# A graph network kernel on one core: the row stores of its three table stages move from GpSimd's DMA queue to SyncE's, behind the loads there

## The chip, the cores and the metric

The kernel runs on one core of a Trainium2 chip. A core has five engines with an instruction queue each: TensorE (PE in the profile), VectorE (DVE), ScalarE (ACT), GpSimd (POOL) and SyncE (SP), and 16 DMA engines that all queues share. SP only issues transfers. The metric is the device time of the kernel in microseconds (us), as the median of several runs.

## The reference

Nodes have rows of 128 numbers. Two relational layers and one attention layer work on the same 400,000 edges, which are sorted by destination. Cut to what matters here:

```python
h = relu(layernorm(x))                        # 12500 x 128
# two layers; relation = argmax of 10 columns of edge_attr
mean[n, r] = mean over edges (src -> n, relation r) of h[src]
h1 = relu(sum_r mean[n, r] @ w_rel1[r] + h @ root1 + b1)
x = x + (the same with h1, w_rel2, root2, b2)
h = relu(layernorm(x))
xl, xr = h @ W_l, h @ W_r
score = leaky_relu(xl[src] + xr[dst]) . att   # 4 heads
x = x + softmax over the edges of dst (score) * xl[src] + bias
```

## The kernel before

The kernel multiplies before it gathers. A table stage (`tables`, L372) computes for each node row all products that edges can ask of it, and an edge pass then gathers one 128-number row of that table per edge. The order of the program is: preparation, `tables("t1")`, edge pass p1, `tables("t2")`, edge pass p2, `tables("t3")`, score pass, softmax weights, `attend`, `finish`. Each is a block of its own, and all engines meet at a barrier between blocks.

A table stage goes over 98 tiles of 128 node rows, in 49 pairs. In a pair number j, buffer k (0 or 1) serves tile i = 2j + k. Every buffer of the stage exists twice, one for even and one for odd tiles: the loaded rows `xt` (t_x in the trace), the normalized rows `hn` (t_hn), their transpose `ht` (t_ht), the product `py` in PSUM (t_py), and the table rows `yb` (t_y) that are stored to HBM. Each engine runs its own stream of instructions, and semaphores tie them together:

- SP loads the rows of x (L420). In t1 the load of tile i waits for the normalized rows of tile i-2 (L489, semaphore s_hn). In t2 it waits for the last addition of tile i-2 (L521, s_yd), since x is added there. In t3 nothing is loaded. SP instead saves x after the relational layers, which lies in A, to `x1_dram` (L440).
- DVE, in its pair j, first makes the rows of pair j+1: statistics (L473, t1 and t3, which in t1 wait for the load), L477, L481, and the normalized rows L489 (in t2 a plain relu, L492). Then, for the two tiles of pair j, it copies the last 256 columns of the product into yb (L511, t1 and t2) and writes A (L516, or L519 and L521, or L514). Before the copy into yb[k] it waits for the store of tile i-2 out of it (s_out).
- ACT takes the square roots (L545), copies the first 1024 columns of the product into yb (L561, all 128 columns in t3; it waits for the same store), and writes ht with a relu (L551).
- PE multiplies tile i (L590, three matmuls of up to 512 columns in t1 and t2, the trace shows each as two), then transposes tile i+2 (L581). A product waits for both copies of tile i-2.
- POOL only issues the stores (L454): tile i goes out when both ACT's and DVE's part of it is done (s_ya and s_yd). A store is 640 KB in t1 and t2 (128 rows of 5,120 bytes) and 64 KB in t3.

A wait on SP or POOL is written as `gate(...)`, and its instructions appear at L81 and L82, lines of that helper. Instructions of one queue are taken in order, so a wait holds up everything behind it.

Of the kernel before, what the change touches and what calls it, by code (L numbers as in the profile page):

```python
# [24 lines left out]
ds = bass.ds  # L25

P = 128
# [7 lines left out]
NT = -(-N // P)  # L35
LAST = N - (NT - 1) * P
# [24 lines left out]
def build(nc, x, src, dst, attr, w_rel1, root1, b1, w_rel2, root2, b2, w_l, w_r, att, bias, out,  # L61
# [3 lines left out]
    def sem(name):  # L65
        return outer.enter_context(nc.semaphore(name))

    def sbuf(stack, name, shape, dt=F32):
        return stack.enter_context(nc.sbuf_tensor(name, shape, dt))
# [6 lines left out]
    def gate(eng, name, *waits):  # L76

        if name not in passed:
            passed[name] = sem(f"gate_{name}")
        for s, v in waits:  # L80
            eng.wait_ge(s, v)  # L81
        eng.sem_inc(passed[name])  # L82

    def load(eng, kind, table, at, n, top):

        _, values = nc.values_load_multi_w_load_instructions(
            table[0:1, ds(at, n)], engines=[kind], min_val=0, max_val=top,
            skip_runtime_bounds_check_because="the tables are clamped where they are made")
        return values
# [20 lines left out]
    with outer:  # L110
# [261 lines left out]
        def tables(name, first, norm, wcols, load_w, bias_in, save_x1):  # L372
# [3 lines left out]
            dest = ytab if nt > D else xltab  # L376
            with ExitStack() as st:
# [8 lines left out]
                yb = [sbuf(st, f"{name}_y{k}", [P, nt]) for k in range(2)]  # L386
# [3 lines left out]
                s_x = [sem(f"{name}_x_in{k}") for k in range(2)]  # L390
# [4 lines left out]
                s_ya, s_yd = sem(f"{name}_copied_act"), sem(f"{name}_copied_dve")  # L395
                s_add = sem(f"{name}_added")
                s_out = [sem(f"{name}_stored{k}") for k in range(2)]
                s_x1 = sem(f"{name}_x1_stored")
                uses_x = first or bias_in is not None
# [9 lines left out]
                def a_tile(i):  # L409
                    return A[:, ds(i * D, D)]  # L410

                with nc.Block() as block:  # L412

                    @block.sync
                    def _(sp):
                        n_w = load_w(sp, wt, brow, s_w)

                        def load(j, k, rows=P):
                            i = 2 * j + k
                            sp.dma_start(xt[k][0:rows, :], x[ds(i * P, rows), :]).then_inc(s_x[k], 16)  # L420

                        def use(j, k):

                            return (s_hn if first else s_yd, 2 * j + k - 1)

                        if uses_x:
                            load(0, 0)
                            load(0, 1)
                            with sp.Fori(1, NT // 2 - 1) as j:
                                for k in range(2):  # L430
                                    gate(sp, "sp", use(j, k))
                                    load(j, k)
                            j = NT // 2 - 1
                            for k in range(2):
                                gate(sp, "sp", use(j, k))
                                load(j, k, P if k == 0 else LAST)
                        elif save_x1:
                            def save(j, k):
                                i = 2 * j + k
                                sp.dma_start(x1_dram[ds(i * P, P), :], a_tile(i)).then_inc(s_x[k], 16)  # L440
                            save(0, 0)
                            save(0, 1)
                            with sp.Fori(1, NT // 2) as j:
                                for k in range(2):

                                    gate(sp, "sp", (s_x[k], 16 * j))
                                    save(j, k)

                    @block.gpsimd
                    def _(pool):  # L450
                        def store(j, k):
                            i = 2 * j + k
                            gate(pool, "pool", (s_yd, i + 1), (s_ya, i + 1))
                            pool.dma_start(dest[ds(i * P, P), :], yb[k][:, :]).then_inc(s_out[k], 16)  # L454
                        with pool.Fori(0, NT // 2) as j:
                            for k in range(2):
                                store(j, k)
                        for k in range(2):
                            pool.wait_ge(s_out[k], 16 * (NT // 2))
                        if save_x1:  # L460
                            for k in range(2):
                                pool.wait_ge(s_x[k], 16 * (NT // 2))

                    @block.vector
                    def _(dve):
# [614 lines left out]
        def finish():  # L1080
            B = 7
            with ExitStack() as st:
# [10 lines left out]
                with nc.Block() as block:  # L1093
# [26 lines left out]
                    def _(dve):  # L1120
# [5 lines left out]
                        for b in range(NT // B):  # L1126
                            k = b % 2
                            dve.wait_ge(s_x[k], 16 * (b // 2 + 1))  # L1128
                            if b >= 2:
# [9 lines left out]
                                            biasb[:, :].rearrange("p (a d) -> p a d", a=1).to_broadcast([P, B, D]), ALU.add).then_inc(s_r, 1)  # L1139

        tables("t1", True, True, ALL, rgcn_weights(w_rel1, root1, b1), b1, False)
        rgcn_pass("p1", True)
        tables("t2", False, False, ALL, rgcn_weights(w_rel2, root2, b2), b2, False)
        rgcn_pass("p2", False)
        relational.close()
        tables("t3", False, True, 2 * D, gat_weights, None, True)
        sc = sbuf(outer, "scores", [P, TILES * H])
        score_pass(sc)
# [39 lines left out]
```

## Time and profile before

| what | value |
|---|---|
| median of 3 runs | 17781.06 us (17738.27 to 17804.8) |
| span of the profiled execution, first to last instruction | 15531.6 us |
| busy in the span | PE 44%, PEld 38%, DVE 42%, ACT 25%, POOL 67% |
| stage t1 | about 953 to 1265 us of the span |
| stage t2 | about 5370 to 5638 us |
| stage t3 | about 9593 to 9830 us |

The profile gives one execution. Its own total time is not on record, only its span, so the 2249.5 us between the span and the median of the runs lie before the first and after the last instruction that the trace shows. The shares of busy time are means over stages that are limited by different things: POOL's 67% is mostly the issue of the gathers in the edge passes. The three table stages together are some 5% of the span. What the change is worth must be read inside them.

### The profile page before, as it was taken

What the parts mean: (1) busy time and instruction counts of PE and PEld (TensorE: products, weight loads), DVE (VectorE), ACT (ScalarE), POOL (GpSimd) and SP (SyncE); (2) the same over time, 40 slices, a digit from 0 to 9 for tenths busy, and PEclk for the clock granted to TensorE, in tenths of its full rate; (3) what the DMA queues carried; (4) which work ended last, traced back from release to release, by engine and by line L of the source; (5) the groups of instructions that cost most, each with busy time, mean ns of one, the idle gap of its engine ahead of it and who ended that gap; (6) DMA issues with size and microseconds to landing.
All of it is one profiled execution on the core that took longest, in us unless ns stands there. A gap on an engine that the chain in (4) does not pass through costs nothing. (4 is left out here: it accounts for less than half of the span.)

```text
span 15531.6 us, 192165 instructions
## 1 busy us (share of the span) xinstructions
PE 6894.7 (44%) x31138; PEld 5952.3 (38%) x31139; DVE 6488.9 (42%) x10730; ACT 3826.4 (25%) x12681; POOL 10415.9 (67%) x10321
## 2 busy tenths in 40 slices
PE   0055444444444564444444444444444444444776
PEld 0023333333333333333333334333333333334775
DVE  3762222222222231111111112566666666667777
ACT  0023222222222232222222222111111111112554
POOL 0125777777777647777777775577777777773665
PEclk9996555555555675555555555555555555557998
DMA  3132111111111241111111112355555555552555
GB/s 129 54 124 96 50 50 50 50 51 50 50 50 50 83 164 52 52 52 52 52 52 52 52 52 60 106 148 148 148 148 148 148 147 148 148 147 84 163 164 162
DMA packets 683413, 1471.04 MB, mean 95 GB/s; under 512 B 193803, under 2 KB 259975, under 8 KB 676759
## 3 DMA queue, kind: packets, MB, share of 16 engines
q0 software_dynamic: 331360, 749.89, 18.2%
q1 hardware_dynamic: 339288, 714.47, 13.9%
q10 hardware_dynamic: 12738, 6.40, 0.1%
q14 instruction: 20, 0.16, 0.0%
q8 instruction: 7, 0.11, 0.0%
HBM read 1117.48 MB, written 352.52 MB: 95 GB/s over the span
## 5 line engine op out<-in xcount | busy, mean ns | idle before, releaser
L694 POOL DMA_INDIRECT p_g<-ytab,p_i x6250 | 6107.0, 977 | 1927.9 <-issue 1691.3
L672 PE MATMUL p_pg<-p_v,p_oh 128*128 x14480 | 3451.5, 425 | 4609.3 <-ACT p_v L732 3432.4
L672 PEld LDWEIGHTS p_pg<-p_v,p_oh 128*128 128x128 f32 x14480 | 3087.5, 320 | 4974.2 <-issue 4974.2
L694 POOL DMA_INDIRECT a_g<-xltab,a_i x3125 | 3205.4, 1026 | 962.7 <-issue 950.9
L647 DVE TENSOR_TENSOR A<-p_pg,A 128x128 f32 x1448 | 422.6, 292 | 6013.8 <-PE p_pg L672 5880.4
L867 PE MATMUL a_pg<-A,a_oh 128*128 x7240 | 1755.6, 431 | 2430.3 <-DVE a_oh L813 2430.3
L867 PEld LDWEIGHTS a_pg<-A,a_oh 128*128 128x128 f32 x7240 | 1577.8, 326 | 2608.2 <-issue 2607.4
L732 ACT ACTIVATE p_v<-p_g,wgt 128x128 f32<-128x128 f32 x6250 | 1960.4, 389 | 461.2 <-issue 437.1
L726 ACT ACTIVATE p_i<-rel_i 128x5 int32 (+1 forms) x1250 | 260.1, 208 | 5338.1 <-DMA p_g<-ytab,p_i 5338.1
L1072 POOL TENSOR_TENSOR s_v<-s_x,scores 128x512 f32<-128x512 f32 x625 | 798.0, 1291 | 660.7 <-PE s_pg L672 415.0
L633 DVE TENSOR_TENSOR p_oh<-cols,local 128x640 f32<-128x640 f32 x1456 | 1199.1, 824 | 38.0 <-PEq L412 12.6
L672 PE MATMUL s_pg<-s_v,s_oh 128*128 x7240 | 957.0, 291 | 314.6 <-DVE A L647 225.1
L672 PEld LDWEIGHTS s_pg<-s_v,s_oh 128*128 128x128 f32 x7240 | 894.6, 199 | 377.1 <-issue 369.1
L790 ACT ACTIVATE a_i<-src_i 128x5 int32 (+1 forms) x625 | 130.1, 208 | 3318.0 <-DMA a_g<-xltab,a_i 3318.0
L813 DVE TENSOR_SCALAR a_oh<-a_dst,node 128x640 f32 x726 | 422.5, 582 | 1251.6 <-ACT a_z L795 1181.3
L633 DVE TENSOR_TENSOR s_oh<-cols,local 128x640 f32<-128x640 f32 x728 | 831.5, 1143 | 0.3 <-PEq L1008 0.3
L1036 ACT ACTIVATE s_v<-s_x,scores 128x32 f32<-128x32 f32 x2500 | 597.3, 309 | 620.4 <-PE s_pg L672 531.3
L826 DVE TENSOR_TENSOR a_z<-a_pg,a_z 128x640 f32 x724 | 597.1, 825 | 203.2 <-issue 192.1
L847 DVE TENSOR_REDUCE scores<-a_leaky 128x640 f32 x724 | 590.5, 816 | 80.9 <-DVE scores L847 80.9
L590 PE MATMUL t_py<-t_w,t_ht 128*128 128x512 f32 (+2 forms) x1568 | 620.7, 539 | 6.5 <-ACT t_ht L551 0.9
L838 DVE TENSOR_TENSOR a_leaky<-a_leaky,attb 128x640 f32<-128x640 f32 x724 | 562.1, 817 | 0.0
L833 DVE SCALAR_TENSOR_TENSOR a_leaky<-a_z 128x640 f32 x724 | 561.4, 816 | 0.0
(167 smaller groups left out, 3395.9 us busy)
## 6 DMA issues: line engine op xcount, KB each, us to landing
a_dst<-in_dst_dram SPq DMA_DIRECT2D x625, 320.0 KB, 4.0
xj_dram<-a_g SPq DMA_DIRECT2D x625, 320.0 KB, 2.2
s_x<-xj_dram SPq DMA_DIRECT2D x625, 320.0 KB, 3.1
ytab<-t_y POOLq DMA_DIRECT2D x196, 640.0 KB, 3.4
p_g<-ytab,p_i POOLq DMA_INDIRECT x6250, 2.5
ea<-in_edge_attr_dram SPq DMA_DIRECT2D x50, 1312.5 KB
a_g<-xltab,a_i POOLq DMA_INDIRECT x3125
t_x<-in_x_dram SPq DMA_DIRECT2D x194, 64.0 KB, 2.0
```

The source lines that it names most:

```text
L590: last = t.matmul(py[k][:, to:to + e - c], ht[k][:, :], wt[:, c:e], start=True, stop=True)
L633: v.tensor_tensor(onehot[k][:, :].rearrange("p (t n) -> p t n", t=G), cols[:, :].rearrange("p (a n) -> p a n", a=1).to_broadcast([P, G, P] ...
L672: last = t.matmul(pg[k][:, 0:width], onehot[k][:, q * P:(q + 1) * P], V[:, ds(at + q * width, width)], start=(q == 0), stop=(q == G - 1))
L694: pool.indirect_dma_start(gbuf[k][:, q * D:(q + 1) * D], None, rows, bass.IndirectOffsetOnAxis(ap=stage[k][:, q:q + 1], axis=0)).then_inc( ...
L732: last = a.activation(V[:, c:c + D], gbuf[k][:, q * D:(q + 1) * D], ACT.Copy, scale=wgt[:, ds(G * g + q, 1)])
L826: v.tensor_tensor(z[k], pg[k][:, 0:GD], z[k], ALU.add).then_inc(s_add, 1)
L833: v.scalar_tensor_tensor(L[k][:, :], z[k], SLOPE, z[k], ALU.mult, ALU.max).then_inc(s_lk, 1)
L838: v.tensor_tensor(lk, lk, attb[:, :].rearrange("p (a d) -> p a d", a=1).to_broadcast([P, G, D]), ALU.mult).then_inc(s_wt, 1)
L847: v.tensor_reduce(sc[:, ds(col[k] * H, G * H)], L[k][:, :].rearrange("p (t c) -> p t c", c=C), AX, ALU.add).then_inc(s_done, 1)
L867: last = t.matmul(pg[k % 2][:, q * D:(q + 1) * D], onehot[k % 2][:, q * P:(q + 1) * P], A[:, ds(at, D)], start=True, stop=True)
L1036: a.activation(to[:, q, h * C:(h + 1) * C], rows[k][:, q * D + h * C:q * D + (h + 1) * C], ACT.Copy, scale=sc[:, ds(G * H * g + q * H + h, ...
L1072: q.tensor_tensor(to[:, 0:m, 0:D].rearrange("p t (h c) -> p t h c", h=H), rows[k][:, 0:m * D].rearrange("p (t h c) -> p t h c", t=m, h=H), ...
```

## The change

The block of POOL in the table stages goes away. SP issues the same stores, of the same sizes, with the same waits, and its stream is written so: in the loop it takes the two loads (or saves) of pair j, and then the two stores of pair j-1. The waits for the last stores at the end of the stage move to SP too. The loads of x, the saves, and what DVE, ACT and PE do stay as they are.

```diff
+                        def store(j, k):
+                            i = 2 * j + k
+                            gate(sp, "sp", (s_yd, i + 1), (s_ya, i + 1))
+                            sp.dma_start(dest[ds(i * P, P), :], yb[k][:, :]).then_inc(s_out[k], 16)
+
+                        def save(j, k):
+                            i = 2 * j + k
+                            sp.dma_start(x1_dram[ds(i * P, P), :], a_tile(i)).then_inc(s_x[k], 16)
+
+                        last = NT // 2 - 1
                         if uses_x:
                             load(0, 0)
                             load(0, 1)
-                            with sp.Fori(1, NT // 2 - 1) as j:
+                            with sp.Fori(1, last) as j:
                                 for k in range(2):
                                     gate(sp, "sp", use(j, k))
                                     load(j, k)
-                            j = NT // 2 - 1
+                                for k in range(2):
+                                    store(j - 1, k)
                             for k in range(2):
-                                gate(sp, "sp", use(j, k))
-                                load(j, k, P if k == 0 else LAST)
-                        elif save_x1:
-                            def save(j, k):
-                                i = 2 * j + k
-                                sp.dma_start(x1_dram[ds(i * P, P), :], a_tile(i)).then_inc(s_x[k], 16)
+                                gate(sp, "sp", use(last, k))
+                                load(last, k, P if k == 0 else LAST)
+                        else:
                             save(0, 0)
                             save(0, 1)
-                            with sp.Fori(1, NT // 2) as j:
+                            with sp.Fori(1, last) as j:
                                 for k in range(2):
-
                                     gate(sp, "sp", (s_x[k], 16 * j))
                                     save(j, k)
-
-                    @block.gpsimd
-                    def _(pool):
-                        def store(j, k):
-                            i = 2 * j + k
-                            gate(pool, "pool", (s_yd, i + 1), (s_ya, i + 1))
-                            pool.dma_start(dest[ds(i * P, P), :], yb[k][:, :]).then_inc(s_out[k], 16)
-                        with pool.Fori(0, NT // 2) as j:
+                                for k in range(2):
+                                    store(j - 1, k)
+                            for k in range(2):
+                                gate(sp, "sp", (s_x[k], 16 * last))
+                                save(last, k)
+                        for j in (last - 1, last):
                             for k in range(2):
                                 store(j, k)
                         for k in range(2):
-                            pool.wait_ge(s_out[k], 16 * (NT // 2))
-                        if save_x1:
-                            for k in range(2):
-                                pool.wait_ge(s_x[k], 16 * (NT // 2))
+                            sp.wait_ge(s_out[k], 16 * (NT // 2))
+                            if not uses_x:
+                                sp.wait_ge(s_x[k], 16 * (NT // 2))
```

On SP's queue the loop of stage t1 stood so before (the name in brackets is the semaphore waited for; t1_rows is s_hn):

```order
23 L420 ISA [waits t1_rows]
24 L420 DMA t_x<-in_x_dram 128x128
25 L420 ISA [waits t1_rows]
26 L420 DMA t_x<-in_x_dram 128x128
27 L429 REGISTER_ALU
28 L429 COMPARE_AND_BRANCH
```

And so it stands in the changed kernel, whose line 429 is the store (t1_copied_dve and t1_copied_act are s_yd and s_ya):

```order
23 L420 ISA [waits t1_rows]
24 L420 DMA t_x<-in_x_dram 128x128
25 L420 ISA [waits t1_rows]
26 L420 DMA t_x<-in_x_dram 128x128
27 L81 ISA
28 L429 ISA [waits t1_copied_dve,t1_copied_act]
29 L429 DMA ytab<-t_y 128x1280
30 L81 REGISTER_ALU
31 L429 ISA [waits t1_copied_dve,t1_copied_act]
32 L429 DMA ytab<-t_y 128x1280
33 L439 REGISTER_ALU
34 L439 COMPARE_AND_BRANCH
```

Each load of the next turn now stands behind two waits for copies and two stores, where nothing stood between.

In stage t2 the same loop of the changed kernel has the loads waiting for t2_copied_dve (s_yd) of tiles 2j-2 and 2j-1:

```order
46 L420 ISA [waits t2_copied_dve]
47 L420 DMA t_x<-in_x_dram 128x128
48 L420 ISA [waits t2_copied_dve]
49 L420 DMA t_x<-in_x_dram 128x128
50 L81 ISA
51 L429 ISA [waits t2_copied_dve,t2_copied_act]
52 L429 DMA ytab<-t_y 128x1280
```

The store of tile 2j-2 now stands behind a load that waits for tile 2j-1. On POOL's queue the stores had the loop for themselves, which read before:

```order
33 L454 ISA [waits t1_copied_dve,t1_copied_act]
34 L454 DMA ytab<-t_y 128x1280
35 L81 REGISTER_ALU
36 L454 ISA [waits t1_copied_dve,t1_copied_act]
37 L454 DMA ytab<-t_y 128x1280
38 L455 REGISTER_ALU
39 L455 COMPARE_AND_BRANCH
```

These rows are gone, in all three stages, and POOL goes from one edge pass to the next.

## Rows read from the trace of the kernel before

**Rows 1.** The page: span, and ACT's group of copies (busy, mean, idle before)

```profile
span 15531.6 us, 192165 instructions
...
L561 ACT ACTIVATE t_y<-t_py 128x1024 f32<-128x1024 f32 (+1 forms) x294 | 227.7, 775 | 339.8 <-PE t_py L590 192.3 <-DMA ytab<-t_y 143.3 <-DMA xltab<-t_y 2.3
```

**Rows 2.** Windows t1, t2, t3: length, busy PE, PEld, DVE, ACT, POOL; PEclk, DMA, GB/s

```profile
953.00:1265.00 312.00, 265.09 (x686) 118.41 (x686) 145.38 (x584) 146.55 (x293) 52.35 (x98) 0.99 0.59 225
5370.00:5638.00 268.00, 260.80 (x686) 118.21 (x686) 111.81 (x392) 117.04 (x196) 52.17 (x98) 0.99 0.69 263
9593.00:9830.00 237.00, 141.27 (x490) 104.91 (x490) 113.82 (x491) 78.97 (x294) 52.78 (x98) 0.50 0.18 55
```

**Rows 3.** Windows of the same kind in `attend` and in edge pass p2

```profile
14200.00:15000.00 800.00, 605.16 (x4537) 566.57 (x4538) 599.18 (x909) 416.86 (x1982) 508.42 (x397) 0.94 0.55 164
...
6000.00:8000.00 2000.00, 878.40 (x3679) 785.31 (x3678) 382.56 (x736) 564.62 (x1908) 1515.77 (x1590) 0.52 0.19 52
```

**Rows 4.** SP's own waits: for whom, us in total, times, longest

```profile
SPq L82 <- DVE t_hn L489: 217.3, 48, 5.8
...
SPq L82 <- DVE A L521: 191.8, 96, 9.3
```

**Rows 5.** Timeline of one pair in t1: start, us, engine, line, [idle before]

```profile
1102.21 0.61 DVE L489 TENSOR_SCALAR t_hn<-t_x,t_mv 128x128 f32<-128x128 f32 x2 [0.17 <-DVE t_mv L481]
...
1102.85 0.30 PE L581 MATMUL t_pt<-ident,t_hn 128*128 128x128 f32 x1 [0.79 <-DVE t_hn L489]
...
1102.93 0.95 SPq L420 DMA_DIRECT2D t_x<-in_x_dram  x2
...
1103.24 2.60 PE L590 MATMUL t_py<-t_w,t_ht 128*128 128x512 f32 x6
...
1106.05 1.02 ACT L561 ACTIVATE t_y<-t_py 128x1024 f32<-128x1024 f32 x1 [2.42 <-PE t_py L590]
...
1106.74 0.49 DVE L473 BATCH_NORM_STATS2 t_st<-t_x 128x6 f32<-128x128 f32 x2
```

**Rows 6.** DVE lines 516, 519: durations, first, last start; line 514's wait (us, times)

```profile
L516 DVE TENSOR_TENSOR A<-t_py,t_b x98: 280/281/283, 959.7 to 1261.9; 128x128 f32 x94, 128x128 f32<-128x128 f32 x4
...
L519 DVE TENSOR_TENSOR A<-t_py,t_b x98: 280/281/282, 5376.8 to 5634.2; 128x128 f32 x94, 128x128 f32<-128x128 f32 x4
...
  DMA x_dram<-A: 11.4, 11
```

**Rows 7.** Lines 420, 454 and 773: from issue to landing

```profile
DMA to landing us min/median/max: 1.7/2.0/3.8
...
DMA to landing us min/median/max: 1.8/3.2/3.5
...
DMA to landing us min/median/max: 2.2/2.2/2.7
```

**Rows 8.** PE's timeline at the start of t1

```profile
954.82 4.41 PE L590 MATMUL t_py<-t_w,t_ht 128*128 128x512 f32 x6 [0.24 <-ACT t_ht L551]
```

**Rows 9.** Timeline in t2: the copies, the last addition, the stores

```profile
5499.98 1.02 ACT L561 ACTIVATE t_y<-t_py 128x1024 f32<-128x1024 f32 x1 [0.75 <-DMA ytab<-t_y]
...
5500.77 0.29 DVE L521 TENSOR_TENSOR A<-A,t_x 128x128 f32 x1
...
5501.31 3.73 SPq L420 DMA_DIRECT2D t_x<-in_x_dram  x2
...
5501.83 0.53 POOL L454 DMA_DIRECT2D ytab<-t_y  x1 [1.41 <-DVE A L521]
...
5503.39 1.02 ACT L561 ACTIVATE t_y<-t_py 128x1024 f32<-128x1024 f32 x1 [2.21 <-DMA ytab<-t_y]
...
5505.30 1.02 ACT L561 ACTIVATE t_y<-t_py 128x1024 f32<-128x1024 f32 x1 [0.72 <-DMA ytab<-t_y]
```

**Rows 10.** SP's saves in t3: two small windows of its timeline

```profile
9639.99 0.97 SPq L440 DMA_DIRECT2D x_dram<-A  x2
...
9641.81 0.34 SPq L440 DMA_DIRECT2D x_dram<-A  x1
```

## The prediction

> **What bounds the kernel now.** I read the page first, then the windows of the three table stages, then the timeline of one pair in t1 and in t2, and last the waits and landings of the queues. The page gives a span of 15531.6 us [rows 1]; the change touches only the stages t1, t2 and t3, 312, 268 and 237 us long [rows 2], so all of it plays in 5% of the span, and what counts is the time of one pair of tiles there, of which each stage has 49.
>
> In t1, DVE's line 516 starts 98 times between 959.7 and 1261.9 us [rows 6]. That is 302.2/97 x 2 = 6.23 us a pair. The timeline shows what closes the cycle [rows 5]. PE ends the product of an odd tile at 1103.24 + 2.60 = 1105.84. ACT copies it from 1106.05 to 1107.07. DVE is done with its part at once and begins the statistics of the next pair at 1106.74, 0.9 us after the product's end. The same steps one pair earlier give the rest: the first normalized rows are done at 1102.21 + 0.35 = 1102.56, PE waits 0.79 us for them, transposes, and starts the odd tile's product at 1103.24, so 0.68 after them. From statistics to these rows are 2.1 us (1106.74 - 6.26 = 1100.48 for the start one pair earlier, to 1102.56). Sum: 0.9 + 2.1 + 0.7 + 2.6 = 6.3, the measured pair. So the chain of DVE, and behind it PE, bounds t1, and the statistics are on it with nothing to spare. The loads are off it only because SP issues them at 1102.93 and 1103.54, right after the normalized rows, and they land 2.0 us later at the median [rows 7], at 1104.9 and 1105.5, so 1.2 us or more before they are needed.
>
> In t2 a pair takes (5634.2 - 5376.8)/97 x 2 = 5.31 us [rows 6]. Both copies of a tile wait for the store two tiles back: ACT's copies at 5499.98, 5503.39 and 5505.30 are all released by the landing of a store [rows 9], and over the kernel such landings cost ACT 143.3 us [rows 1]. The cycle of one yb buffer is: copy begins, DVE's last addition ends at 5500.77 + 0.29 = 5501.06 (1.1 us), POOL issues at 5501.83 (0.8 us), the store lands (3.2 to 3.5 us [rows 7]), next copy 0.1 later. That is 5.3, the measured pair. So t2 is bound by its stores, and the two buffers run this cycle side by side.
>
> In t3 PE is busy 60% at half the clock, a pair takes 237/49 = 4.8 us, DMA has a share of 0.18 [rows 2], and only 11.4 us are lost to a transfer, a save [rows 6].
>
> **The change in t1.** POOL's two issues a pair, 0.53 us each, go; SP has room for them, since it waits 217.3 us for normalized rows [rows 4]. But the loads of the next pair now stand behind the store of the odd tile, which waits for ACT's copy of it. From the end of the odd product (0):
> - ACT's copy ends at 1.23 (0.21 + 1.02, [rows 5]).
> - SP issues the store 0.37 after its release, as it issues a load at 1102.93 for rows done at 1102.56: 1.60.
> - SP goes round its loop and issues the first load. Two issues within a turn are 0.61 apart (0.95 - 0.34). Across the end of a turn I have 9639.99 + 0.63 = 9640.62 to 9641.81, 1.2 with a small wait in it [rows 10]. I take 1.05: 2.65, and the second load at 3.26.
> - They land after 2.0 at the median, 1.7 at least [rows 7]: 4.65 and 5.26. The store of 640 KB is ahead of them on the same queue; it lands 3.2 after 1.60, at 4.8, so the first load hardly comes before that. I take 4.8 and 5.25.
> - Statistics at 4.9 instead of 0.9. The second tile's load is a little late, which costs 0.1 more.
>
> That is +4.1 a pair: 10.35 us. It hits rows 2 to 48 of the loop, 47 pairs: 47 x 4.1 = +193 us.
>
> PE's clock adds to it. PE is busy 265.09/312 = 85% in t1, at a granted 0.99, which is 2.4 GHz [rows 2]. After the change it would do 0.85 x 6.23 = 5.3 us in 10.35, 51%, with an idle stretch of over 4 us each pair. At 60% in t3 the grant is 0.50 (1.2 GHz) [rows 2], at 44% in p2 0.52, at 76% in `attend` 0.94 [rows 3]. At the lower level the product takes 4.41 us instead of 2.60 [rows 8], and with the slower transpose the pair 2.0 more: 12.35, +6.1. But PE would then be busy some 80% again, which goes with the high clock. So I expect both levels in turn, and the product behind the idle stretch, the one on the chain, mostly at the lower. I take +5.3: **+249 us**; bounds +193 and +287. The Trainium skill says the same of idle gaps while waiting for a DMA (*TensorE: Matmul & The Clock Gate*, HAM oscillation — how this bites in real kernels); no run here has yet shown it in this loop.
>
> **The change in t2.** The loads and stores wait for nearly the same thing, but the store of tile 2j-2 now stands behind a load that waits for the last addition of tile 2j-1. So both buffers' stores go out together. From that addition's end (0):
> - SP issues the load at 0.25 (5501.06 to 5501.31, [rows 9]), the first store at 0.25 + 0.61 = 0.86, the second at 1.5.
> - The first lands after 3.2 [rows 7], at 4.1. The second is moved behind it: two landings stand 1.9 apart (5503.39 and 5505.30 [rows 9]), so at 6.0.
> - Copy 0.1 later, last addition 1.1 later: 7.2.
>
> Against 5.31 that is +1.9 a pair, 47 x 1.9 = **+89 us**. The gain of SP's quicker issue (0.25 against POOL's 0.77) is in it. If a store of SP lands quicker, the nearest row is L773 with 320 KB and 2.2 [rows 7]; 320 KB more at half of the 1.9 gives 3.15, almost the same. Bounds: +1.3 a pair (60 us) to +2.5 (118 us). PE, busy 260.8/268 = 97% of t2 now [rows 2], would be busy 0.97 x 5.31/7.2 = 72%, near `attend`, so I leave its clock.
>
> **The change in t3.** Four issues a pair on SP take 3 x 0.61 + 1.05 = 2.9 of the 4.8 us. The saves of pair j+1 go out about a pair before DVE overwrites their source; they land long before. The cover is 1.9 us; if it were gone, each us of it costs 49. The 11.4 us may come back. I take **0**, -11 to +10.
>
> **The sum.** 249 + 89 + 0 = +338 us on the span of 15531.6, which gives 15870. The span lies 2249.5 below the median of the runs, and I leave that difference alone: 17781 + 338 = 18119, so **18120 us**. Bounds: 193 + 60 - 11 = +242 and 287 + 118 + 10 = +415.
>
> **Rivals.**
> - *The stores gain from the faster queue, and the order costs nothing* (not slower). Place: the yb cycle in t2. The release-to-issue time falls from 0.77 to 0.25 and the landing perhaps by 0.1: -0.6 x 49 = -30 us, 17750. For it: t2 is bound by this cycle. Against it: it needs the even store to leave before the odd tile is done, while the load ahead of it waits for exactly that; it decides only if that wait is shorter than the 0.5 us gained, and the copies of the two tiles stand 1.9 us apart. 4%. The skill's table of issuing engines names Sync for a simple store and calls that path generally faster (*DMA: Bandwidth & Descriptors*, Issuing engine by pattern); by that rule alone the change would be this gain.
> - *Only the issue moves, no time* (17781). SP sits idle enough [rows 4]: 294 issues x 0.34 = 100 us in three stages. It needs the loads in t1 to have over 4 us to spare; they have 1.2. 4%. The same page says under Issuing engines are not separate DMA queues that issuing from several engines saves only sequencer time; by it nothing else would change.
> - *Only one of the two loops suffers*: t2 alone +89 (17870) or t1 alone +249 (18030). 7%.
> - *Both suffer more than I sum*: PE stays at 1.2 GHz in t1 and falls to it in t2 as well (4.41 a product, over 10 us a pair there, +4.5): 287 + 220 = +507, 18290. Against it: at that level PE is busy all the time in t2, which goes with the high grant. 6%.
> - The forecast, both loops longer by +180 to +510: 79%.
>
> **How the numbers follow.** Range: from +180 to +500, 17960 to 18280, which holds the bounds of the sum and some 8 in 10 of the chance. A measurement of this kernel tells about 0.5%, 89 us, from no change. Slower by more than that: the forecast, the heavier case, and nearly all of the one-loop case, 92%. Within it: the two rivals without loss and a light t2 alone, 7%. Faster by over 0.5% would take 89 us out of the stages, which no term gives: 1%.
>
> **What the profile after would show.** In t1, DVE's statistics (L473) wait some 4 us for the landing of t_x in each pair, where now they follow the addition at once; SP's waits name ACT's copy; line 516's first and last start are some 500 to 550 us apart; PEclk lies between 0.5 and 0.9. In t2, two stores are issued 0.6 us apart on SP, ACT's copies wait for their landings, and a pair takes about 7.2 us with PEclk above 0.9. In t3 nothing but the place of the stores changes. Edge passes and `attend` keep their lengths. I am wrong if the loads in t1 land before 1 us, if the two stores of t2 leave apart, or if the gathers, now first on POOL's queue, run otherwise than before.

## The result, and the profile after

The changed kernel takes **18089.25 us** (median of 4 runs, 18044.45 to 18107.5), the kernel before 17759.67 us (4 runs, 17735.79 to 17804.8) beside it. The ratio is 1.0178, 95% interval [1.0157, 1.0200]: slower by 330 us, that is 1.8%, and clear of the noise. Forecast were 18120 us and +338.

The page of the kernel after gives a span of 18105.7 us where [rows 1] have 15531.6. The time of this same execution was 18107.5 us. So nothing to speak of lies around the span, and the 2249.5 us that the prediction put there must be something else; this is taken up with the whole kernels below.

```profile
span 18105.7 us, 191823 instructions
...
ytab<-t_y SPq DMA_DIRECT2D x196, 640.0 KB, 3.0
```

The stores stand in SP's name, and their median time from issue to landing is 3.0 us. The page of the kernel before has 3.4 for the same 640 KB from POOL (the 3.2 of [rows 7] is the median of all stores of that line, with the small ones of t3):

```profile
ytab<-t_y POOLq DMA_DIRECT2D x196, 640.0 KB, 3.4
```

The windows of t1, t2 and t3 show where the time went; columns as in [rows 2]:

```profile
953.00:1558.00 605.00, 373.22 (x686) 161.25 (x686) 149.28 (x584) 146.63 (x293) 0.00 (x0) 0.78 0.31 117
6236.00:6569.00 333.00, 253.89 (x682) 117.39 (x680) 111.04 (x388) 116.48 (x194) 0.00 (x0) 0.99 0.54 212
11183.00:11420.00 237.00, 141.25 (x490) 104.90 (x490) 114.19 (x492) 79.55 (x299) 0.53 (x1) 0.50 0.19 55
```

t1 went from 312 to 605 us at a granted clock of 0.78 for 0.99, t2 from 268 to 333, t3 kept its 237. More exactly by the first and last start of the lines that write A (now L520, L523 and L518; for the first two [rows 6] give 302.2 and 257.4 us):

```profile
L520 DVE TENSOR_TENSOR A<-t_py,t_b x98: 280/281/282, 959.8 to 1554.8; 128x128 f32 x94, 128x128 f32<-128x128 f32 x4
...
L523 DVE TENSOR_TENSOR A<-t_py,t_b x98: 280/281/282, 6239.2 to 6565.3; 128x128 f32 x94, 128x128 f32<-128x128 f32 x4
...
L518 DVE COPY A<-t_py x98: 291/292/293, 11188.5 to 11416.3; 128x128 f32 x94, 128x128 f32<-128x128 f32 x4
```

That is 595.0 us in t1, +293; 326.1 us in t2, +69; 227.8 us in t3, as before.

Why t1 is longer is seen in one pair of its timeline (columns as in [rows 5]):

```profile
1205.43 0.61 DVE L493 TENSOR_SCALAR t_hn<-t_x,t_mv 128x128 f32<-128x128 f32 x2 [0.17 <-DVE t_mv L485]
...
1206.51 4.99 PE L594 MATMUL t_py<-t_w,t_ht 128*128 128x512 f32 x6
...
1211.44 2.53 PE L594 MATMUL t_py<-t_w,t_ht 128*128 128x512 f32 x6
...
1211.70 1.02 ACT L565 ACTIVATE t_y<-t_py 128x1024 f32<-128x1024 f32 x1 [4.70 <-PE t_py L594]
...
1214.11 0.97 SPq L420 DMA_DIRECT2D t_x<-in_x_dram  x2
...
1216.38 0.63 DVE L477 BATCH_NORM_STATS2 t_st<-t_x 128x6 f32<-128x128 f32 x2 [4.00 <-DMA t_x<-in_x_dram]
```

The product that follows the wait runs 4.99 us and ends at 1211.50. ACT's copy ends at 1212.72, SP issues the next loads at 1214.11, and DVE's statistics start at 1216.38 after 4.00 us of waiting for them: 4.88 us after the product's end, where [rows 5] have 0.9. The next product takes 2.53 us. This is one of the longer pairs, 12.79 us from statistics to statistics where the mean of the stage is 12.27. The slow product is not always as slow. In the timeline of the stage the 47 products behind such a wait take 3.88 to 5.03 us, 4.69 in the mean; none takes the 2.60 us of [rows 5].

SP's own waits have changed their names. Normalized rows cost it 217.3 us in [rows 4] and now 5.8. ACT's copy (at the store of the odd tile) and DVE's row of A (at the store of the even tile) have taken their place:

```profile
SPq L82 <- ACT t_y L565: 245.5, 51, 5.5
SPq L82 <- DVE A L520: 206.4, 47, 4.8
...
SPq L82 <- DVE t_hn L493: 5.8, 1, 5.8
```

In t2 the two stores of a pair leave together, the second issue 0.7 us after the first. The second copy of each pair is released by the landing of its store. For the first the profile names PE's product, which is about as late:

```profile
6403.40 1.03 ACT L565 ACTIVATE t_y<-t_py 128x1024 f32<-128x1024 f32 x1 [0.39 <-DMA ytab<-t_y]
...
6404.20 0.29 DVE L525 TENSOR_TENSOR A<-A,t_x 128x128 f32 x1
...
6405.46 1.06 SPq L429 DMA_DIRECT2D ytab<-t_y  x2
...
6408.58 1.02 ACT L565 ACTIVATE t_y<-t_py 128x1024 f32<-128x1024 f32 x1 [3.98 <-PE t_py L594]
...
6410.14 1.02 ACT L565 ACTIVATE t_y<-t_py 128x1024 f32<-128x1024 f32 x1 [0.37 <-DMA ytab<-t_y]
```

From the addition's end (6404.49) the stores leave 0.97 later, the first copy starts 3.12 after that, the second 1.56 behind it.

There is one part of the change that the prediction did not have. At the end of a block, ahead of the barrier, each engine runs an instruction that the trace calls DRAIN. GpSimd's is the one that matters here. These are its three in the table stages, of before and after (durations in ns, then first and last start):

```profile
L412 POOLq DRAIN  x3: 8056/8056/8062, 1266.7 to 9829.6; - x3
```

```profile
L412 POOLq DRAIN  x3: 46/47/47, 945.2 to 11183.6; - x3
```

Before, each began when the stage's other work was done (1266.7, right after t1) and the barrier waited 8 us for it. After, it takes 0.05 us and lies at the stage's start. Three times 8.0 is 24 us less, and all that lies between the last row of a stage and the next stage's start, or the next pass's, is 28 us less. So the sum is 293 + 69 + 0 - 28 = +334, against +330 measured.

### The profile page after: what moved, and what is told of

The parts are those of the page before. It is cut to its first block and busy times, and to the rows that moved or that the text cites. A ratio compares the mean times of both kernels' runs of the same rounds, so it can differ in the third digit from the quotient of the medians.

```text
span 18105.7 us, 191823 instructions
## 1 busy us (share of the span) xinstructions
PE 6686.7 (37%) x31138; PEld 5584.0 (31%) x31139; DVE 6384.5 (35%) x10730; ACT 3601.1 (20%) x12681; POOL 10166.0 (56%) x10027
## 5 line engine op out<-in xcount | busy, mean ns | idle before, releaser
L676 PE MATMUL p_pg<-p_v,p_oh 128*128 x14480 | 3155.4, 363 | 6127.8 <-issue 4812.9
L676 PEld LDWEIGHTS p_pg<-p_v,p_oh 128*128 128x128 f32 x14480 | 2695.0, 264 | 6589.1 <-issue 6580.5
L698 POOL DMA_INDIRECT a_g<-xltab,a_i x3125 | 3151.5, 1008 | 2236.0 <-issue 919.3
L799 ACT ACTIVATE a_z<-a_g 128x640 f32<-128x640 f32 x625 | 460.4, 737 | 4585.5 <-issue 2495.4
L676 PE MATMUL s_pg<-s_v,s_oh 128*128 x7240 | 945.8, 289 | 326.8 <-DVE A L651 250.3
L594 PE MATMUL t_py<-t_w,t_ht 128*128 128x512 f32 (+2 forms) x1568 | 721.4, 610 | 74.8 <-ACT t_ht L555 74.5
L594 PEld LDWEIGHTS t_py<-t_w,t_ht 128*128 128x128 f32 x1568 | 338.7, 250 | 394.3 <-issue 393.8
```

What stands on the lines that cost most here:

```text
L594: last = t.matmul(py[k][:, to:to + e - c], ht[k][:, :], wt[:, c:e], start=True, stop=True)
L676: last = t.matmul(pg[k][:, 0:width], onehot[k][:, q * P:(q + 1) * P], V[:, ds(at + q * width, width)], start=(q == 0), stop=(q == G - 1))
L698: pool.indirect_dma_start(gbuf[k][:, q * D:(q + 1) * D], None, rows, bass.IndirectOffsetOnAxis(ap=stage[k][:, q:q + 1], axis=0)).then_inc( ...
```

## The experiments

The theory is that the order on SP's queue makes the loss: loads and stores stand behind waits that are released late, and TensorE's clock falls in the gap that this opens in t1. The main rival is that the queue makes it: loads and stores of SP share one queue, and the 640 KB of a store hold up the loads behind it. The rival to the clock's share is that t1 lengthens by the wait alone, and the slower clock costs nothing since PE waits anyway.

Nine kernels of the twelve are cut: they keep the preparation, the three table stages and `finish`, and leave out both edge passes, the score pass, the softmax weights and `attend`, with A set to ones before `finish`. One execution is some 1,900 us, so that the changes of t1 and t2 are some 16% and 3% of it. These kernels are compared with each other by time, and stage by stage by the lines that write A. In every kernel of mine each value that an engine reads from a table into a register is also held at 0 or above, which adds a few register instructions; so they are compared with each other and not with the two kernels above.

```diff
-        rgcn_pass("p1", True)
         tables("t2", ...)
-        rgcn_pass("p2", False)
         tables("t3", ...)
-        score_pass(sc)
-        softmax_weights(sc)
-        attend(sc)
+        with nc.Block() as block:
+            @block.vector
+            def _(dve):
+                nc.vector.memset(A[:, :], 1.0)
```

**The two kernels, cut** (the edit above, on before and on after).

> This kernel leaves out the two edge passes, the score pass, the softmax weights and attend, and fills A with ones before finish, so that preparation, the three table stages of the kernel before and finish remain, some 2 ms. It is the base for the kernels below, which leave out the same. Both theories: stages t1, t2 and t3 keep their lengths of before, 6.2, 5.3 and 4.8 us a pair.

> The same cut, with the table stages of the changed kernel. If the whole loss lies in the table stages: +362 us over tables_before, of it 293 in t1 (12.27 against 6.23 us a pair) and 69 in t2 (6.72 against 5.31), which is somewhat more than the +330 us between the medians of the whole kernels. If part of the change's time lies in the edge passes, whose gathers now find POOL's queue unused by stores: another number, by what it is off.

Measured: 1886.16 us (1885.57 to 1890.02) and 2214.90 us (2213.64 to 2215.63), +328.7, where +362 was expected: the ends of the stages were still left out then, and t2 lost 61 us here, not 69. By the lines that write A, t1 went from 302.1 to 595.7 us, t2 from 264.5 to 325.3, t3 228.1 and 228.1. The gap from t1's last row to t2's first shrank from 25.1 to 15.5, the next from 18.1 to 9.1. So the whole difference of the full kernels is made in these stages, and the edge passes have no part in it.

```profile
L517 DVE TENSOR_TENSOR A<-t_py,t_b x98: 280/281/282, 962.8 to 1264.9; 128x128 f32 x94, 128x128 f32<-128x128 f32 x4
```

```profile
L521 DVE TENSOR_TENSOR A<-t_py,t_b x98: 280/281/283, 962.2 to 1557.9; 128x128 f32 x94, 128x128 f32<-128x128 f32 x4
```

**The order without the queue.** POOL stores again, as before; SP still waits for both copies where its stores stood, but issues nothing there.

```diff
                         def store(j, k):
                             i = 2 * j + k
                             gate(sp, "sp", (s_yd, i + 1), (s_ya, i + 1))
-                            sp.dma_start(dest[ds(i * P, P), :], yb[k][:, :]).then_inc(s_out[k], 16)
...
+                        def pstore(j, k):
+                            i = 2 * j + k
+                            gate(pool, "pool", (s_yd, i + 1), (s_ya, i + 1))
+                            pool.dma_start(dest[ds(i * P, P), :], yb[k][:, :]).then_inc(s_out[k], 16)
```

> SP waits for both copies of pair j-1 behind its loads, as in the changed kernel, but issues no store; POOL issues all stores as before. My theory, that the order of the waits delays the loads of t1: t1 keeps nearly all of its loss, about 11.7 us a pair (0.6 less than with the stores: SP's issue of 0.35 goes, and the loads have no 640 KB ahead of them), and t2 is back at 5.3; in all +265 us over tables_before. Rival, that sharing one queue of transfers is what delays the loads: t1 back near 6.3 us a pair, +0 to +30 us.

Measured: 2209.52 us (five runs at 2208.24 to 2209.64, one at 2253.84), +323 over the cut kernel of before. With the stores on a queue of their own, the loss of t1 is still there, and more than that, so the theory that the loads suffer because they share the store's queue falls for t1; the place behind the wait decides. But the size was missed by 58 us, since t1 did not gain at all:

```profile
L532 DVE TENSOR_TENSOR A<-t_py,t_b x98: 280/281/283, 961.2 to 1586.7; 128x128 f32 x94, 128x128 f32<-128x128 f32 x4
```

That is 625.5 us, 12.9 a pair, +323 over the cut kernel of before and 30 us more than with everything on SP. One pair shows how:

```profile
1201.51 0.53 POOL L473 DMA_DIRECT2D ytab<-t_y  x1 [4.99 <-ACT t_y L577]
...
1203.66 0.29 DVE L489 BATCH_NORM_STATS2 t_st<-t_x 128x6 f32<-128x128 f32 x1 [3.24 <-DMA t_x<-in_x_dram]
...
1205.37 0.29 DVE L489 BATCH_NORM_STATS2 t_st<-t_x 128x6 f32<-128x128 f32 x1 [1.42 <-DMA t_x<-in_x_dram]
```

The first load comes earlier behind the odd product than in the kernel after, but the second is now 1.42 us late, where both statistics ran together there. POOL's store of 640 KB starts in the same microsecond as the loads, so the likely reason is that the bytes of the second load go along with it on the same 16 DMA engines; that is argued, no run isolates it. In t2 this kernel takes 262.8 us, about as the cut kernel of before (264.5): there the stores on POOL are free of SP's order again, and the +61 of the kernel after is gone. So in t2 it is the stores' place that costs, not the loads'.

**TensorE kept busy.** The kernel after, with 5 more matmuls of 384 columns behind the even product of each pair of t1, whose result nobody reads.

```diff
                                 last.then_inc(s_mm, 1)
+                                if first and k == 0 and not tail:
+                                    for _ in range(5):
+                                        t.matmul(pt[0][:, P:512], ident[:, :], wt[:, 0:512 - P], start=True, stop=True)
```

> tables_after with more work: in t1, PE does five matmuls of 384 columns behind each even product, 0.64 us each at the high clock, into a part of PSUM that nobody reads. They lie where PE waits for the rows of the next pair. 
Measured: 2128.73 us (2123.74 to 2149.59), 86 us less than the cut kernel after, with more work. (The profiled run is the longest of the six. Its t1 begins at 986.2 us for 962.2, so what it has more lies ahead of the table stages.) The windows of t1, of the cut kernel after and of this one:

```profile
955.00:1561.00 606.00, 372.51 (x686) 161.70 (x686) 149.52 (x584) 146.63 (x293) 0.00 (x0) 0.78 0.31 116
```

```profile
980.00:1496.00 516.00, 426.55 (x1166) 212.09 (x1166) 148.50 (x581) 146.76 (x292) 0.00 (x0) 0.98 0.36 137
```

The granted clock goes from 0.78 to 0.98, that is 2.4 GHz nearly throughout. PE sat idle for 4.90 us ahead of the slow product in the kernel after; with the fillers 1.69 and 1.84 us of that are left in the pairs shown. The product behind the wait runs 2.60 us instead of 4.99, with the fillers after the other product:

```profile
1200.67 2.60 PE L595 MATMUL t_py<-t_w,t_ht 128*128 128x512 f32 x6
...
1205.58 3.39 PE L599 MATMUL t_pt<-t_w,ident 128*128 128x384 f32 x10
```

This splits t1's +293 into its two terms. With the clock up t1 takes 506.5 us, 10.44 a pair, so 204 us are the order's and 89 (595.7 - 506.5) are the clock's, 1.84 us of each pair (12.28 - 10.44). The Trainium skill has this as a rule (*TensorE: Matmul & The Clock Gate*, HAM oscillation — how this bites in real kernels): a matmul loop with idle gaps while it waits for a DMA falls back to the slower clock. The trace agrees: a grant of 0.78 with the gap, 0.98 with most of it filled.

**One stage at a time.** The kernel before, with SP's stream of the kernel after (left out in the diff) and no POOL block in one stage only: t1, t2 or t3.

```diff
+                        if name == "t1":
...
+                            return
...
+                    if not (name == "t1"):
                     @block.gpsimd
```

> The same cut to preparation, table stages and finish; the stores of t1 alone are on SP, t2 and t3 are as before. My theory, that the stages' losses add and that each stage ends about 9 us sooner when POOL has issued no DMA in it (GpSimd's drain at the end of the block, 8.06 against 0.03 us in the runs so far): +294 - 9 = +285 us over tables_before (1886). Rival, that t1 and t2 hurt each other or that the shorter ends come from something else: another number than 285.

> The same with t2 alone on SP: +61 - 9 = +52 us over tables_before, 6.74 us a pair against 5.44. Rival, that SP's quicker issue helps t2: at most the same time as tables_before.

> The cut to preparation, table stages and finish, with t3 alone on SP. My theory: t3 keeps 4.77 us a pair, and only its drain goes: 9 us less than tables_before, 1877. Rival, that four issues a pair crowd SP: t3 over 4.9 us a pair.

Measured: 2159.71 us (2157.53 to 2167.48), +273.5; 1939.46 (1938.83 to 1943.62), +53; 1875.74 (1873.22 to 1877.44), -10.4. Expected were +285, +52 and -9. The three add up to +316, against +329 with all at once. Most of what is missing is in t2: in the first of these kernels t2 takes 257.0 us, though nothing in it is changed against the cut kernel of before with 264.5. In the full kernel of before it takes 257.4. Why t2 differs by 7 us between kernels in which its own code is the same stays open. t3 alone keeps its rows (1570.9 to 1798.8, 4.70 us a pair before as after) and gains the drain at its end. In the kernel with t2 alone two of the three drains are long:

```profile
L413 POOLq DRAIN  x3: 34/8056/8064, 1267.3 to 1854.6; - x3
```

They take 8.06 us; the one of the stage without stores on POOL takes 0.03.

**The same stores on SP in another order.** In t1 the loads run a pair further ahead, so that a load never stands behind the copy whose product needs it; in t2 each store goes ahead of the load that waits for the same addition.

```diff
                         if first:
                             ...
+                            with sp.Fori(1, last - 1) as j:
+                                for k in range(2):
+                                    gate(sp, "sp", use(j + 1, k))
+                                    load(j + 1, k)
+                                for k in range(2):
+                                    store(j - 1, k)
                         elif uses_x:
                             with sp.Fori(1, last) as j:
                                 for k in range(2):
-                                    gate(sp, "sp", use(j, k))
+                                    store(j - 1, k)
                                     load(j, k)
```

> All stores on SP, in another order: in t1 the loads of pair j+1 stand ahead of the stores of pair j-1, in t2 each store stands ahead of the load that waits for the same addition. My theory, that the order costs the time and the queue doesn't: t1 back at 6.25 us a pair, t2 at 5.3, and the ends of the stages 9 us shorter: 30 to 38 us less than tables_before, about 1853. Rival, that the loads and stores on one queue delay each other in DMA whatever their order: t1 and t2 stay over 6.8 and 6 us a pair, more than tables_before.

Measured: 1867.59 us as the median of five runs with two values, about 1844.5 and 1868; about 1853 was expected. In the profiled run, one of the longer, t1 begins 22 us later (983.5 for 962), so this difference lies in the preparation, ahead of all stages. The stages give -42 against the cut kernel of before:

```profile
L537 DVE TENSOR_TENSOR A<-t_py,t_b x98: 280/281/281, 983.5 to 1285.3; 128x128 f32 x94, 128x128 f32<-128x128 f32 x4
...
L540 DVE TENSOR_TENSOR A<-t_py,t_b x98: 279/281/281, 1300.5 to 1550.8; 128x128 f32 x94, 128x128 f32<-128x128 f32 x4
```

t1 is back at 301.8 us, 6.22 a pair, and t2 at 250.3 (5.16 a pair, below the 5.31 of [rows 6]). The same bytes on the same queue cost nothing, so the queue as such is not what made the kernel slower. What is left to gain is small: 7 us in t2 against the full kernel's 257.4, and the drains. In t2 PE is then busy for 250 of the 251 us (window 1300 to 1551), so the stores no longer bound that stage. This bears on the rule that the prediction weighed (the Trainium skill, *DMA: Bandwidth & Descriptors*, Issuing engines are not separate DMA queues: several issuing engines save only issue time). As a statement on bytes it fits; what the kernel lost is the order of waits on one sequencer.

**A single transfer on POOL.** The reordered kernel, with one load of 512 bytes by POOL at each stage's start.

```diff
+                    @block.gpsimd
+                    def _(pool):
+                        pool.dma_start(pd[:, :], base_dram[0:P].rearrange("(a p) -> a p", a=1)).then_inc(s_pd, 16)
+                        pool.wait_ge(s_pd, 16)
```

> tables_reordered, and POOL loads 512 bytes once at the start of each table stage and waits for them. If GpSimd's drain at the end of a block takes its 8 us whenever POOL has issued any DMA, however long ago: +24 us over tables_reordered, three drains of 8 us. If it takes them only for transfers that have just ended, or in proportion to their number: the time of tables_reordered.

Measured: 1846.38 us (1845.12 to 1847.49), the shorter of the reordered kernel's values.

```profile
L415 POOLq DRAIN  x3: 113/123/130, 951.6 to 1536.8; - x3
```

The drain grew from 0.03 to 0.12 us and no more. One small load at the start of a stage does not make the 8 us. The stages with 98 stores have them, and their size makes no difference: with the 64 KB stores of t3 the drain is as long as with the 640 KB of t1 and t2. Whether it is their number, or that the last one has only just ended, no run here separates.

**The full kernels.**

> The whole kernel before, with one more register operation behind each number that is loaded from the tables (it is kept at zero or above), as the base for the two below, which have it too. Both theories: within 1% of the kernel before. It also gives a second trace of the edge passes, whose lengths differ between the two profiled executions so far (span 15531.6 before, 18105.7 after).

> The whole changed kernel with the same register operations. If the loss lies in the table stages and their ends alone: +329 us over whole_before_clamped, as in the cut kernels (2214.9 - 1886.2), whatever the edge passes take on this chip. If the edge passes take part: a number that differs from 329 by over 60 us.

> The whole kernel with all stores on SP in the other order. My theory: 42 us less than whole_before_clamped (14 us in t2, 3 x 9 us of drains; the cut kernels gave 1886 against 1843 to 1869), 0.25%, at the edge of what can be told. Rival, that the drains' 9 us come back in the whole kernel, where the next block is an edge pass: 14 us less or nothing.

Measured, each with its ratio to the kernel before: 17886.27 us, 1.0023 [1.0012, 1.0033]; 18225.24, 1.0209 [1.0193, 1.0226]; 17853.03, 1.0006 [0.9995, 1.0018]. So the change costs +339 here (+329 was expected), and the reordered kernel is 33 us (0.2%) below its own counterpart, for 42 expected. The 33 fit 7 in t2 and 27 for the three ends; the expectation had 14 for t2, from the cut kernels. A gain of 0.2% is at the edge of what these measurements can tell.

The passes in between keep their lengths. From the last row of t1 to the first of t2 the two clamped kernels have 4763.8 us (before) and 4753.6 (after), from t2 to t3 4675.9 and 4673.5, and behind t3 6684 and 6698. The gathers show no sign of running otherwise now that no stores of the table stages go ahead of them on POOL's queue. But since the passes differ by up to 14 us between two traces, the 9 us of a stage's end do not show there one by one; it is the medians that fit them, +339 where the rows of t1 and t2 alone give +361.

They also answer what the 2249.5 us were. On one chip the kernel before took 15550.07 us (15539.31 to 15586.13, 11 runs), on others 17882.78 (9 runs) and 17853.67 (23 runs). The trace of [rows 1], with its span of 15531.6, fits the first kind; the timed runs the second. The table stages do not differ between them: 302.2 us for t1 in [rows 6] and here

```profile
L517 DVE TENSOR_TENSOR A<-t_py,t_b x98: 280/281/282, 960.4 to 1262.6; 128x128 f32 x94, 128x128 f32<-128x128 f32 x4
```

What runs between and behind them does. These are the windows of p1, of the kernel before and of its full counterpart on the other chip:

```profile
1265.00:5370.00 4105.00, 1727.37 (x7240) 1545.30 (x7240) 1001.61 (x2181) 1110.51 (x3755) 3125.81 (x3125) 0.52 0.18 50
```

```profile
1265.00:6020.00 4755.00, 1525.89 (x7240) 1352.35 (x7240) 940.21 (x2181) 1027.65 (x3755) 3043.00 (x3125) 0.59 0.15 43
```

The same 7240 matmuls and 3125 gathers take 650 us longer, with every engine busy for less time. This pair of traces also differs by the register instructions. The trace of the kernel after does not have them, and is of the slower kind too: between its table stages lie 4678 us (p1) and 4614 (p2), behind t3 6685, where the kernel before has 4105, 3955 and 5701. That is 573 + 659 + 984 = 2216 us, nearly all of the 2249.5.

PE's waits at the product of the gathered rows show how the passes were held up, but one line alone misleads (over the whole kernel: us, times, longest):

```profile
PE p_pg L672 <- ACT p_v L732: 3432.4, 919, 24.9
...
PE p_pg L672 <- issue: 1021.7, 271, 5.5
```

```profile
PE p_pg L673 <- issue: 4559.6, 2347, 16.6
```

In the second trace ACT is named for only 160.9 us, so most of what "issue" (nothing that the profile shows) has gained was ACT's before. Over all names this idle time grows from 4609 to 6254 us. What lies behind it on those chips stays open.

## Why the prediction was right, and where its steps were off

- **The verdict and the mechanism** held. In t1 the loads wait behind the odd tile's copy, in t2 the even store behind the odd addition; both loops suffer, t3 doesn't. The two rivals that had the change cost nothing are out by the timeline of after, and the one in which only one loop suffers by the cut kernels of one stage each, +273.5 and +53 us.
- **t1, the order**: 4.9 us from the product's end to the statistics was forecast, 4.88 measured, and with the clock up a pair takes 10.44 us for the forecast 10.35. The term is 204 us, forecast 193.
- **t1, the clock**: this term was too small. The forecast had 1.2 us a pair of at most 2.0 (56 us on top of the 193, and 287 as the bound of the whole stage), since the product behind the wait was expected at the lower level mostly, but not always. It measured 1.84 us a pair, 89 in all, and the stage +293, just past that bound; its 595 us from first to last row lie outside the 500 to 550 that the prediction named as a sign. Two steps were off. The product behind the wait takes 4.69 us in the mean of all 47, and none kept the full clock throughout. And the 4.41 us of [rows 8], taken as the price of the lower level, were a product whose last matmuls already ran faster: the slowest products of t1 take 5.03, twice the 2.53 of a product at 2.4 GHz, so those are at 1.2 GHz from end to end. The product after the slow one, at 2.53 us in the pair shown, shows that the clock does come back within the pair.
- **t2**: +89 forecast, +69 measured, 6.72 us a pair for 7.2. The term off is the distance of the two landings, taken as 1.9 from two stores of POOL [rows 9]. Two stores that leave 0.7 us apart on SP let their copies start 1.56 apart. The first copy starts 3.12 after the store's issue, about as forecast (3.2), but PE's product is as late as the landing there: the profile names PE as the last releaser. PE's clock stayed up in t2 (0.99), as forecast.
- **t3**: 0 forecast, 0 measured. The 11.4 us that might have come back are 7.6 us in 46 waits for saves, with no gain in the stage.
- **Not seen**: the ends of the stages, -28 us, 24 of them the drains. They stood in the trace of before; I had read the insides of the stages only. With +44 in t1 and -20 in t2 against the forecast, they leave the sum 4 us off, so that it came out as near as that is in part luck: errors that cancel.
- **Wrong**: that 2249.5 us lie around the span. They lie inside it, in the edge passes and behind t3: the trace of before was of a quick execution and the timed runs were longer ones, as they are on the other chips. It did no harm only because the table stages take the same time on both.

## What to carry to other kernels

When an issue is moved to another queue, write down what each instruction of that queue waits for, in order, and ask of every load whether it now stands behind a wait that is released later than the load has to leave. In this kernel the stores could share a queue with the loads at no cost once the loads ran one step further ahead (t1), or once the waits stood in the order in which they are released (t2). And look at the ends of blocks too: what an engine does before a barrier is part of the price of giving it work.

## What the hardware showed that I had not expected

- GpSimd's DRAIN at the end of a block took 8.05 to 8.06 us when that block issued 98 stores, 0.12 with a single small load, 0.03 to 0.05 with none. After an edge pass with 3125 gathers it took 22 us in the trace of before (first row below), and 11 to 22 in the other full kernels. There it costs nothing, since DVE's DRAIN starts later than GpSimd's ends (second row; 5337.9 + 22.7 is 5360.6). Why it takes as long as it does is not shown.

```profile
L711 POOLq DRAIN  x2: 21820/22275/22730, 5337.9 to 9566.5; - x2
...
L711 DVEq DRAIN  x2: 693/706/718, 5364.6 to 9592.2; - x2
```

- 3.4 us more matmul work in each pair of t1 made the stage 89 us shorter.
- The same kernel takes 15550 us on one chip and 17850 to 17880 on others. The difference lies in the edge passes and behind t3, none of it in the table stages.
- With the stores back on a queue of their own, and the loads behind the same waits, t1 took 30 us longer than with all of it on one queue.
